# MoE weight buffers of 1 MB instead of 512 KB, and every second weight load issued from GpSimd

## What is computed

```python
# layer 0
xn = layernorm(x)
x = x + window_attention(xn) + moe(xn)
# layer 1
xn = layernorm(x)
x = x + retention(xn) + ternary_ffn(xn)

def moe(x):                       # D=1024, F=4096, E=8, every expert on every token
    for ei in range(8):
        h = gelu(x @ W1[ei] + b1[ei])
        y = h @ W2[ei] + b2[ei]
        out = out + y * (gate * (idx == ei))[:, None]

def ternary_ffn(x):               # W_fc, W_proj reduced to -1, 0, 1 first
    h = layernorm(gelu(x @ absmean(W_fc).T))
    return h @ absmean(W_proj).T
```

## Time and profile before

| | us |
|---|---|
| median of 2 runs | 10197.33 |
| the two runs | 10128.99 and 10265.67 |
| profiled execution | 9734.86 |
| its span on the slowest core | 9733.3 |
| its spans on the 8 cores | 9706.3 to 9733.3 |

### The profile page before, as it was taken

One profiled execution on the slowest core, in us unless ns is written; L12 is line 12 of the kernel. 1 busy time (PEld: TensorE's weight loads), 2 busy tenths in 40 slices (PEclk: granted clock), 3 DMA queues, 4 the chain that ended last, 5 costly groups with the idle time before them and its releaser, 6 DMA issues.

```text
span 9733.3 us, 84307 instructions; the slowest of 8 cores (9706.3 to 9733.3 us)
## 1 busy us (share of the span) xinstructions
PE 6575.5 (68%) x27956; PEld 2824.2 (29%) x27956; DVE 2606.6 (27%) x4154; ACT 1642.7 (17%) x2701; POOL 313.2 (3%) x414
## 2 busy tenths in 40 slices
PE   4545546477777999999999996555555551015777
PEld 2323323233333344444444442111111220001222
DVE  4233232300000101111010113555555554432111
ACT  1122121211111121111212112111111110001111
POOL 0000101011111000000000000000000000000000
PEclk6656656589999999999999998777777775557998
DMA  1311303099999644444444442111111113422222
GB/s 37 33 15 20 35 0 35 5 200 209 206 204 208 177 154 146 149 147 150 151 145 152 147 151 74 36 26 26 26 25 24 25 23 118 138 74 67 86 78 95
DMA packets 580680, 929.87 MB, mean 96 GB/s; under 512 B 180111, under 2 KB 393615, under 8 KB 576162
## 3 DMA queue, kind: packets, MB, share of 16 engines
q1 hardware_dynamic: 276706, 739.88, 22.3%
q0 software_dynamic: 303552, 184.60, 15.6%
HBM read 949.54 MB, written 159.38 MB: 114 GB/s over the span
## 4 chain that ended last, share of the span: by engine, by line
PE 52%; DVE 19%; DMA 17%; issue 6%; ACT 5%; DVEq 1%; SPq 0%; POOL 0%; ACTq 0%; POOLq 0%
PE psE L1102 7%; PE psF L1102 7%; PE psC L1056 7%; PE psD L1056 7%; DMA arena_bf<-w 5%; DMA arena_bf<-w2lay 3%; DMA w1sc<-arena_bf 2%; DVE arena_f L828 2%; DMA arena_f<-wfcT 2%; DMA w2sc<-arena_bf 2%; DMA arena_f<-wprojT 2%; DVE arena_f L851 1%; PE psC L1657 1%; PE psD L1657 1%; PE psF L1732 1%
## 5 line engine op out<-in xcount | busy, mean ns | idle before, releaser
L1056 PE MATMUL psC<-xn,arena_bf 128*128 128x512 bf16 x4096 | 1010.8, 391 | 192.7 <-DMA arena_bf<-w 182.2
L1102 PE MATMUL psE<-arena_bf 128*128 128x512 bf16 x4096 | 933.0, 387 | 107.9 <-DMA arena_bf<-w2lay 72.6
L1056 PE MATMUL psD<-xn,arena_bf 128*128 128x512 bf16 x4096 | 988.4, 385 | 0.0
L1102 PE MATMUL psF<-arena_bf 128*128 128x512 bf16 x4096 | 910.3, 379 | 26.8 <-DMA arena_bf<-w2lay 24.9
L1117 DVE TENSOR_TENSOR arena_f<-psE,arena_f 128x512 f32<-128x512 f32 x128 | 88.5, 692 | 2869.1 <-PE psE L1102 2869.1
L1071 ACT ACTIVATE arena_bf<-psC,b1lay_s 128x512 bf16<-128x512 f32 x512 | 351.9, 687 | 2696.5 <-PE psC L1056 2696.5
L1056 PEld LDWEIGHTS psC<-xn,arena_bf 128*128 128x128 bf16 x4096 | 399.4, 100 | 721.2 <-issue 284.7
L1102 PEld LDWEIGHTS psE<-arena_bf 128*128 128x128 bf16 x4096 | 402.7, 99 | 626.3 <-issue 174.2
L1056 PEld LDWEIGHTS psD<-xn,arena_bf 128*128 128x128 bf16 x4096 | 408.2, 100 | 508.5 <-issue 44.8
L1102 PEld LDWEIGHTS psF<-arena_bf 128*128 128x128 bf16 x4096 | 398.4, 98 | 520.2 <-issue 47.3
L1071 ACT ACTIVATE arena_bf<-psD,b1lay_s 128x512 bf16<-128x512 f32 x512 | 351.8, 687 | 550.6 <-PE psD L1056 550.5
(11 more groups left out here) (320 smaller groups left out, 7279.9 us busy)
## 6 DMA issues: line engine op xcount, KB each, us to landing
arena_bf<-w1sc SPq DMA_DIRECT2D x384, 512.0 KB, 3.5
arena_bf<-w2sc SPq DMA_DIRECT2D x384, 512.0 KB, 4.6
arena_bf<-w POOLq DMA_DIRECT2D x128, 512.0 KB, 13.2
w1sc<-arena_bf SPq DMA_DIRECT2D x128, 512.0 KB, 8.0
arena_bf<-w2lay POOLq DMA_DIRECT2D x128, 512.0 KB, 10.5
w2sc<-arena_bf SPq DMA_DIRECT2D x128, 512.0 KB, 8.8
arena_f<-wfcT SPq DMA_DIRECT2D x64, 512.0 KB, 4.7
arena_f<-wprojT SPq DMA_DIRECT2D x64, 512.0 KB, 4.3
```

The lines of the kernel that those rows point to most:

```text
L1056: p.op("pe", (lambda w1u, kc, fc, t0, psb: lambda e: e.matmul(psb[:, 0:512], w1u[:, kc * 256 + fc * 128: kc * 256 + (fc + 1) * 128], CH(K. ...
L1102: p.op("pe", (lambda w2u, fkl, fk, psb: lambda e: e.matmul(psb[:, 0:512], w2u[:, fkl * 128:(fkl + 1) * 128], h_all[:, fk * 512:(fk + 1) * ...
```

## The change

Four things, of which the first three are in `emit_moe`:

- The scratch `w1sc` and `w2sc` is laid out in units of [128, 4096] instead of [128, 2048].
- W1 and W2 come in 8 loads of 1 MB for each expert instead of 16 of 512 KB, into two buffers of 1 MB instead of four of 512 KB. A W1 load covers four blocks, a W2 load the whole of one block; all 32 matmuls of a W2 block wait for its one load. The stores of group 0 double in size and halve in number in the same way.
- In groups 1 to 3, loads of odd number are issued from GpSimd and those of even number from SP.
- In `emit_l1_ffn` the loads of odd number (`wqfc_sc` and `wqproj_sc`) are issued from GpSimd too. Their size and buffers stay.

The matmuls, their order and all work on the other engines are the same.

```diff
-    K.w1sc = dt_("w1sc", [8, 16, 128, 2048], BF16, kind="Internal").ap()
-    K.w2sc = dt_("w2sc", [8, 8, 2, 128, 2048], BF16, kind="Internal").ap()
+    K.w1sc = dt_("w1sc", [8, 8, 128, 4096], BF16, kind="Internal").ap()
+    K.w2sc = dt_("w2sc", [8, 8, 128, 4096], BF16, kind="Internal").ap()
...
-    w1b = K.bpool.alloc(4 * 2048)
-    w2b = K.bpool.alloc(4 * 2048)
+    w1b = K.bpool.alloc(2 * 4096)
+    w2b = K.bpool.alloc(2 * 4096)
...
-            for fb in range(16):
-                slot = u1 % 4
+            for fb in range(8):
+                slot = u1 % 2
                 u1 += 1
-                w1u = w1b[:, slot * 2048:(slot + 1) * 2048]
+                w1u = w1b[:, slot * 4096:(slot + 1) * 4096]
                 if g == 0:
                     src = K.ins["w1"][e8].rearrange(
-                        "(kc p) f -> p kc f", p=128)[:, :, fb * 256:(fb + 1) * 256]
-                    dstv = w1u.rearrange("p (kc f) -> p kc f", f=256)
+                        "(kc p) f -> p kc f", p=128)[:, :, fb * 512:(fb + 1) * 512]
+                    dstv = w1u.rearrange("p (kc f) -> p kc f", f=512)
...
-                    wt = p.dma("sp", (lambda w1u, e8, fb: lambda e: e.dma_start(
-                        w1u, K.w1sc[e8][fb]))(w1u, e8, fb),
+                    wt = p.dma("sp" if fb % 2 == 0 else "gp",
+                        (lambda w1u, e8, fb: lambda e: e.dma_start(
+                            w1u, K.w1sc[e8][fb]))(w1u, e8, fb),
                         deps=[w1war[slot], K.w1sc_tok[(e8, fb)]])
-                for fc in range(2):
-                    hidx = fb * 2 + fc
+                for fc in range(4):
+                    hidx = fb * 4 + fc
...
-                    if fc == 1:
+                    if fc == 3:
...
             for dc in range(8):
-                for h2 in range(2):
-                    slot = u2 % 4
-                    u2 += 1
-                    w2u = w2b[:, slot * 2048:(slot + 1) * 2048]
...
+                slot = u2 % 2
+                u2 += 1
+                w2u = w2b[:, slot * 4096:(slot + 1) * 4096]
+                if g == 0:
+                    src = K.ins["w2lay"][e8][dc]
+                    wt = p.dma("gp", (lambda w2u, src: lambda e: e.dma_start(
+                        w2u, src))(w2u, src), deps=[w2war[slot]] + pre)
+                else:
+                    wt = p.dma("sp" if dc % 2 == 0 else "gp",
+                        (lambda w2u, e8, dc: lambda e: e.dma_start(
+                            w2u, K.w2sc[e8][dc]))(w2u, e8, dc),
+                        deps=[w2war[slot], K.w2sc_tok[(e8, dc)]])
...
-                dep0 = [wts2[0], ps.gate(bank)] + hdone
+                dep0 = [wt, ps.gate(bank)] + hdone
...
+                if g == 0:
+                    stok_ = p.dma("sp", (lambda w2u, e8, dc: lambda e:
+                        e.dma_start(K.w2sc[e8][dc], w2u))(w2u, e8, dc), deps=[wt])
+                    K.w2sc_tok[(e8, dc)] = stok_
+                    w2war[slot] = [mmtok, stok_]
...
-            wt = p.dma("sp", (lambda dstv, src: lambda e: e.dma_start(
-                dstv, src))(dstv, src), deps=[w1war[slot]] + fc_done + pre)
+            wt = p.dma("sp" if fb % 2 == 0 else "gp",
+                (lambda dstv, src: lambda e: e.dma_start(
+                    dstv, src))(dstv, src), deps=[w1war[slot]] + fc_done + pre)
...
-            wt = p.dma("sp", (lambda w2u, dc: lambda e: e.dma_start(
+            wt = p.dma("sp" if dc % 2 == 0 else "gp",
```

More of the change, by code:

```diff
@@ L1008, in emit_moe @@
     h_all = K.bpool.alloc(32 * 512)
-    w1b = K.bpool.alloc(4 * 2048)
-    w2b = K.bpool.alloc(4 * 2048)
+    w1b = K.bpool.alloc(2 * 4096)
+    w2b = K.bpool.alloc(2 * 4096)
     cbc = K.fpool.alloc(2 * 512)
     tmp = K.fpool.alloc(512)
-    w1war = [None] * 4
-    w2war = [None] * 4
+    w1war = [None, None]
+    w2war = [None, None]
     cbcwar = [None, None]
@@ L1056, in emit_moe @@
                         p.op("pe", (lambda w1u, kc, fc, t0, psb: lambda e: e.matmul(
-                            psb[:, 0:512], w1u[:, kc * 256 + fc * 128: kc * 256 + (fc + 1) * 128],
+                            psb[:, 0:512], w1u[:, kc * 512 + fc * 128: kc * 512 + (fc + 1) * 128],
                             CH(K.xn, kc, t0, 512),
@@ L1078, in emit_moe @@
             for dc in range(8):
-                wts2 = []
-                units = []
-                for h2 in range(2):
-                    slot = u2 % 4
-                    u2 += 1
-                    w2u = w2b[:, slot * 2048:(slot + 1) * 2048]
[L1085 to L1094, removed]
+                slot = u2 % 2
@@ L1095, in emit_moe @@
                 bank = "E" if dc % 2 == 0 else "F"
                 psb = K.psE if dc % 2 == 0 else K.psF
-                dep0 = [wts2[0], ps.gate(bank)] + hdone
+                dep0 = [wt, ps.gate(bank)] + hdone
                 for fk in range(32):
[L1099 to L1103, removed]
+                    p.op("pe", (lambda w2u, fk, psb: lambda e: e.matmul(
+                        psb[:, 0:512], w2u[:, fk * 128:(fk + 1) * 128],
@@ L1104, in emit_moe @@
                         h_all[:, fk * 512:(fk + 1) * 512],
-                        start=(fk == 0), stop=(fk == 31)))(w2u, fkl, fk, psb),
-                        deps=dd)
+                        start=(fk == 0), stop=(fk == 31)))(w2u, fk, psb),
+                        deps=dep0 if fk == 0 else [])
                 mmtok = p.sig("pe")
[L1108 to L1116, removed]
+                if g == 0:
[3 more added lines that the diff above has]
+                    w2war[slot] = [mmtok, stok_]
+                else:
+                    w2war[slot] = mmtok
@@ L1723, in emit_l1_ffn @@
             w2u = w2b[:, slot * 4096:(slot + 1) * 4096]
-            wt = p.dma("sp", (lambda w2u, dc: lambda e: e.dma_start(
-                w2u, K.wqproj_sc[dc].flatten_outer_dims() if False
-                else K.wqproj_sc[dc].rearrange("p k d -> p (k d)")))(w2u, dc),
+            wt = p.dma("sp" if dc % 2 == 0 else "gp",
+                (lambda w2u, dc: lambda e: e.dma_start(
+                    w2u, K.wqproj_sc[dc].rearrange("p k d -> p (k d)")))(w2u, dc),
                 deps=[w2war[slot]] + pr_done)
```

## The result

The changed kernel is slower by 0.7%: ratio 1.0069 with an interval of 1.0048 to 1.0089, from 9738 to 9769 us before and 9787 to 9867 after. Executions in which the cores of a die (0 to 3, or 4 to 7) ran at a lower granted clock are left out of every ratio, and such cores out of the stage means of the experiments; with them the medians are 9961 before and 10151 after. The profiled execution has a span of 9811.0 us against 9733.3.

A forecast was written before the change was run, and what follows sets the result against it. Group 0 was taken as bound by DMA engines or buffers, groups 1 to 3 by TensorE alone. Between -85 (engines) and +11 (buffers) it took -20, plus 0 + 0, giving 10180 us from 10197; range 10060 to 10340.

The forecast's parts named there:

- two buffers are too few: Rival, group 0: each unit exposes landing and hold, up to +126 us, about 10290; 15%, and 4% for over 2%.
- Part 1: Group 0: same bytes in half as many transfers with longer rows, 85 us less if the engines alone set the pace.
- Part 2: Group 0: two buffers instead of four, pace (landing + hold) / 2 a unit, +11 us if buffers set the pace.
- the engine reading: Group 0: DMA engines alone set the pace, so fewer packets bring -85 us.
- the buffer reading: Group 0: the release of the two buffers sets the pace, 164.8 us per expert against 163.4, +11 us for eight.
- landing: Group 0: engine time of a load and the other buffer's store plus 2.6 us fixed: 11.9 us W1, 12.1 W2.
- The slow start after a wait: Group 0: after a wait PE runs mostly at the lower clock, 32 matmuls taking 8.75 us instead of 7.
- Part 3: Groups 1 to 3: every second load from POOL lands in 5.3 us, needed after 6.4; cost 0, upper bound 19 us.
- Part 4: Last feed-forward: odd loads from POOL stay hidden behind units of at least 6.9 us; cost 0.
- The packet price: Group 0 loads: a packet costs 1.1 ns of engine time, from W1 units of 2048 packets against W2's 256.
- memory, not packets: Rival, group 0: memory bytes are the limit, so shorter packet counts bring 0 and +11 us is left, 10210; 20%.

The follow-up runs named there:

- split_only: Kernel before (four 512 KB buffers) with every second load without a cast, MoE and last feed-forward, issued from POOL: ratio 1.0012 (0.9995 to 1.0030).
- ring5: Changed kernel with all castless loads from SP, W1 and W2 sharing five 1 MB buffers: group 0 1311 us, ratio 0.9970 (0.9902 to 1.0037), slower chip.
- ring10_half: Kernel before with W1 and W2 sharing ten 512 KB buffers: group 0 1320 us on cores 4 to 7, ratio 1.0012 (0.9956 to 1.0068), slower chip.
- w1_three: Changed kernel with all castless loads from SP and three 1 MB W1 buffers instead of two: group 0 1323 us, 9759 and 9764 us, slower chip.
- w1lay: Kernel before with W1 stored on the host in load order (4 KB rows): group 0 1259 us, ratio 0.9922 (0.9880 to 0.9964), slower chip.

## Why the prediction was wrong

*Direction.* I forecast -20 us and said groups 1 to 3 stay; both were wrong in the same direction, and the whole is +67 (0.69% of 9735). The rival that came true is "two buffers are too few", for which I had worked out up to +126.

*Part 1 was right in size and worth nothing.* DMA queues of the changed kernel in a W1 phase (2615 to 2695 us) and a W2 phase (2705 to 2770), against the earlier trace rows:

```profile
q0 software_dynamic: 6857, 7.57, 70.5%
q1 hardware_dynamic: 1000, 7.30, 22.7%
...
q0 software_dynamic: 869, 6.35, 61.8%
q1 hardware_dynamic: 880, 6.40, 23.7%
```

W1's engine time is 0.705 x 80 / 7.57 = 7.5 us per MB (8.8 before, 7.7 forecast). But the two queues add up to 0.93 and 0.86 of the time, from 1.14 and 1.00: the engines did not carry more, they stood idle more. The step that failed is the one at the end of Part 2, where I mixed the engine reading (-85) into the buffer reading (+11). They are not two estimates to be averaged: the slower of them sets the time. Without the mixing the forecast would have been +11, of the right sign and a quarter of the measured 45; the rest is the landing, below. The Trainium skill (DMA: Bandwidth & Descriptors, "Rules for kernel authors") advises at least 1 MB per DMA for full bandwidth; by it the change should have helped. In this kernel the 512 KB loads already filled the engines, so the larger ones had nothing to fill.

*Part 2 was the right mechanism, too small.* PE in order of time in an expert of group 0, against the earlier trace rows (rows in between are left out):

```profile
2614.52 3.57 PE L1057 MATMUL psC<-xn,arena_bf 128*128 128x512 bf16 x8 [4.83 <-DMA arena_bf<-w]
...
2636.45 3.57 PE L1057 MATMUL psC<-xn,arena_bf 128*128 128x512 bf16 x8 [5.15 <-DMA arena_bf<-w]
...
2658.82 3.57 PE L1057 MATMUL psC<-xn,arena_bf 128*128 128x512 bf16 x8 [6.30 <-DMA arena_bf<-w]
...
2720.21 9.94 PE L1096 MATMUL psE<-arena_bf 128*128 128x512 bf16 x32 [5.08 <-DMA arena_bf<-w2lay]
2729.98 7.07 PE L1096 MATMUL psF<-arena_bf 128*128 128x512 bf16 x32
2740.97 9.80 PE L1096 MATMUL psE<-arena_bf 128*128 128x512 bf16 x32 [3.92 <-DMA arena_bf<-w2lay]
```

I had the two buffers in turn, one landing while the other is in use. In fact they bunch: PE uses both back to back, 64 matmuls, then waits 4 to 6 us with nothing, at 21.9 and 22.4 us a pair in W1, 20.8 in W2. That is 11.1 a unit in W1 (10.55 forecast) and 10.4 in W2 (10.65). The term that was mis-sized is W1's landing: 13.9 us, forecast 11.9, probably since the two loads, issued 7 us apart (2625.06 and 2631.97 in this expert), share the engines and the stores. W2's was 11.4, forecast 12.1. With the measured landings the same sum gives (11.55 + 10.3) x 8 - 4.8 = 170 us an expert, +53 for eight, near the 45. But it puts most of this on W1, where the runs found +21 for W1 and +28 for W2, so how the phases share the loss stays open. The slow start after a wait was as forecast: 3.57 us for 8 matmuls instead of 1.89.

*Part 3* put 0 on the queue and gave 19 us as its upper bound; it is 12 to 14. PE in the changed kernel's groups 1 to 3, and the loads issued when a W2 unit starts (core 5; other engines left out):

```profile
3480.07 7.07 PE L1096 MATMUL psE<-arena_bf 128*128 128x512 bf16 x32
3480.83 0.53 POOL L1089 DMA_DIRECT2D arena_bf<-w2sc  x1 [13.28 <-PE psF L1096]
3486.98 7.07 PE L1096 MATMUL psF<-arena_bf 128*128 128x512 bf16 x32
3487.28 0.32 SPq L1089 DMA_DIRECT2D arena_bf<-w2sc  x1
```

POOL's issue starts 0.76 us after the unit, SP's 0.30, and these are the medians on all eight cores. In the middle of a phase the load then lands in 5.1 to 5.3 us from POOL, forecast 5.3, and in 4.8 to 5.0 from SP. So the median load from POOL is there 1.0 us before PE needs it, where one from SP has some 1.7, and my 0 was right for the median. What I left out is the spread: depending on the core, one load in ten takes more than 5.6 to 6.5 us, from either queue, and the longest 6.0 to 7.5. With POOL's 0.7 us less in hand more of these are late, and with two buffers each late one is a wait. PE's waits for loads are 10 us of this core's 18; the rest is not in its list of waits and was not traced further. The Trainium skill's rule that several issuing engines gain no bandwidth (DMA: Bandwidth & Descriptors, "Rules for kernel authors") agrees: split_only stands at 1.0012.

*Part 4* was right: the last feed-forward did not move on six cores, with the same two buffers and half of its loads from POOL, as I had argued from a unit's having more work there, which no run tested.

*The packet price* (1.1 ns) held for the queue's share (7.5 us per MB, 7.7 forecast) but not for time: 1 KB rows brought at most 9 us where it says 70, and 4 KB rows 45 to some 75 instead of 110. So the "memory, not packets" rival was half right.

## What to carry to other kernels

Fewer, larger buffers of the same total bytes are not free: count how many units may be landing, in use and being stored at once, and do not go below that. When a stage waits for transfers, first look whether the queues are full; if they are, a larger transfer cannot help, and the lever is to use each loaded byte for more work (here -3.6%) or to lay the source out in long rows (-0.8%). When two mechanisms each give a pace, take the slower one, not a value in between.

## What the runs showed of the hardware

- Under many queued transfers neighbouring cores can part. In the traced execution of ring5 group 0 took 1319 to 1329 us on cores 0, 2, 4 and 6 and 1297 to 1301 on 1, 3, 5 and 7; in ring10_half it took 1334 and 1337 on cores 4 and 6 and 1310 and 1299 on 5 and 7. It is not always the even one: other executions of ring5 have spans of 9719 us on core 0 and 9748 on core 1, where the traced one has 9747 and 9720. On the same chip w1_three (1318 to 1326) and w1lay (1255 to 1264) show no such split. The Trainium skill (HBM Reference, "Specifications (TRN2)") says that two cores share a memory domain; why neighbours are unequal under load was not tried.
- From the start of a PE unit that frees a buffer to the start of the next issue it was 0.76 us on POOL and 0.30 on SP. The landing of 1 MB without a cast then took 0.1 to 0.4 us more from POOL in the middle of a phase. The medians over all loads do not show this: they are 5.9 and 5.8 us for POOL against 5.0 and 5.4 for SP on core 5, but 5.3 and 5.2 against 5.8 and 5.6 on core 1. At 512 KB (split_only, core 0, W2) it was 5.0 against 3.4.
- Group 0 moves 403 MB of memory traffic in 1303 us, 309 GB/s per core with all eight at it; with W1 in long rows 403 / 1259 = 320 GB/s (on the slower chip).
